# Decoder layer on one core: attention scores transposed by pairs of query tiles, the maximum over keys spread by products of ones with a diagonal

## The reference

```python
q = jnp.einsum('bsd,ed->bse', x, Wq)
k = jnp.einsum('btd,ed->bte', context, Wk)
v = jnp.einsum('btd,ed->bte', context, Wv)
dots = jnp.einsum('bse,bte->bst', q, k) * scale
attn = jax.nn.softmax(dots, axis=-1)
out = jnp.einsum('bst,bte->bse', attn, v)
```

## Time and profile before

| | us |
|---|---|
| median of three runs | 405.06 |
| lowest and highest | 404.93, 406.09 |
| span of the profiled execution | 403.8 |
| attention, from its first score matmul to its last query product | 82.0 to 284.9 |

### The profile page before, as it was taken

One profiled execution on the slowest core, in us unless ns is written; L12 is line 12 of the kernel. 1 busy time (PEld: TensorE's weight loads), 2 busy tenths in 40 slices (PEclk: granted clock), 3 DMA queues, 4 the chain that ended last, 5 costly groups with the idle time before them and its releaser, 6 DMA issues.

```text
span 403.8 us, 7801 instructions
## 1 busy us (share of the span) xinstructions
PE 395.0 (98%) x2584; PEld 367.1 (91%) x2584; DVE 300.1 (74%) x1093; ACT 237.8 (59%) x519; POOL 215.9 (53%) x209
## 2 busy tenths in 40 slices
PE   8999999999999999999999999999999999999877
PEld 7878888899999999999999999999788899999766
DVE  5797768786757867476864848572986989899996
ACT  3886859454764466464545434342557977779462
POOL 1788999764385333153430300000166858989993
PEclk9999999999999999999999999999999969999999
DMA  7900213004434312233211000000100000000102
GB/s 226 310 2 1 83 55 102 8 11 128 128 89 121 118 30 59 58 84 104 65 47 30 2 0 2 1 2 2 27 1 2 0 2 2 28 28 27 41 28 67
DMA packets 19992, 21.38 MB, mean 53 GB/s; under 512 B 3180, under 2 KB 16624, under 8 KB 19952
## 3 DMA queue, kind: packets, MB, share of 16 engines
q1 hardware_dynamic: 18832, 19.96, 16.5%
q10 hardware_dynamic: 1120, 0.92, 0.7%
HBM read 18.78 MB, written 2.10 MB: 52 GB/s over the span
## 4 chain that ended last, share of the span: by engine, by line
PE 80%; POOL 12%; DVE 4%; issue 3%; DMA 1%; ACT 0%; SPq 0%; DVEq 0%; POOLq 0%; ACTq 0%
PE keep_pQ L75 11%; PE keep_pQ L76 11%; PE keep_pQ L77 11%; POOL ffn_prod L1258 9%; PE context_pA L1051 6%; PE context_pA L1053 6%; PE context_pA L1052 6%; PE context_pR L1085 6%; PE context_pR L533 3%; PE context_pA L533 3%; POOL ffn_near L1326 2%; PE ffn_pK L1807 2%; PE context_pR L75 2%; PE context_pR L77 2%; PE context_pR L76 2%
## 5 line engine op out<-in xcount | busy, mean ns | idle before, releaser
L899 DVE TENSOR_TENSOR att_pTl<-context_pR,att_pTh 128x512 fp32r<-128x512 f32 x64 | 36.9, 586 | 29.8 <-ACT att_pTh L811 29.5
L811 ACT ACTIVATE att_pTh<-context_pR 128x512 fp32r<-128x512 f32 x64 | 32.1, 514 | 40.1 <-PE context_pR L1085 40.1
L1258 POOL TENSOR_TENSOR ffn_prod<-ffn_first,ffn_near 128x1024 f32<-128x1024 f32 (+1 forms) x29 | 54.1, 1885 | 2.1 <-DVE ffn_first L1684 2.1
L851 ACT ACTIVATE att_prob<-keep_pQ,att_nmax 128x1206 f32<-128x1206 f32 x16 | 20.3, 1269 | 35.9 <-DVE att_nmax L935 35.8
L930 DVE TENSOR_REDUCE att_mx<-keep_pQ 128x1 f32<-128x402 f32 x64 | 34.5, 564 | 6.9 <-PE keep_pQ L77 6.6
L1837 PE MATMUL ffn_pT<-keep_ident,ffn_prod 128*128 128x128 f32 x240 | 30.5, 283 | 3.7 <-POOL ffn_prod L1258 3.7
L1837 PEld LDWEIGHTS ffn_pT<-keep_ident,ffn_prod 128*128 128x128 f32 x240 | 28.6, 148 | 5.8 <-DVE ffn_hT L1717 4.8
L786 POOL TENSOR_TENSOR keep_rstd<-att_ve,keep_mhalf 128x4 f32<-128x4 f32 x3 | 3.0, 1007 | 55.9 <-DVE att_ve L989 55.9
L1085 PE MATMUL context_pR<-keep_ident,att_prob 128*128 128x128 f32 (+1 forms) x208 | 31.8, 272 | 0.2 <-DVE att_pTl L899 0.2
L1051 PE MATMUL context_pA<-att_pTh,att_cNh 128*128 128x256 f32 (+1 forms) x104 | 31.0, 298 | 0.0
L1051 PE MATMUL context_pA<-att_pTh,context_cNh 128*128 128x256 f32 (+1 forms) x104 | 30.9, 297 | 0.0
(11 more groups left out here) (336 smaller groups left out, 1300.3 us busy)
## 6 DMA issues: line engine op xcount, KB each, us to landing
keep_raw<-in_ctxT SPq DMA_DIRECT2D x24, 256.0 KB, 2.7
keep_raw<-in_ctx SPq DMA_DIRECT2D x24, 256.0 KB, 3.0
out<-keep_x SPq DMA_DIRECT2D x16, 128.0 KB, 1.7
keep_x<-in_x SPq DMA_DIRECT2D x3, 512.0 KB, 9.9
gru_wout<-in_W_out SPq DMA_DIRECT2D x1, 512.0 KB, 8.7
keep_raw<-in_fWq SPq DMA_DIRECT2D x2, 256.0 KB
keep_raw<-in_ctxT SPq DMA_DIRECT2D x8, 32.5 KB, 3.1
keep_raw<-in_ctx SPq DMA_DIRECT2D x4, 65.0 KB
```

The lines of the kernel that those rows point to most:

```text
L811: act.activation(to, bank, ACT.Copy).then_inc(bank_high, 1)
L899: dve.tensor_tensor(to, bank, half(it, 0, n)[0].bitcast(F32), ALU.subtract).then_inc(bank_free, 1)
L1258: return eng.tensor_tensor(prod[:, i % PB, a:b].rearrange("p h (i j) -> p h i j", j=KEYS), (factor if factor is not None else first[:, n % ...
```

## The change

`stage_attention` is rewritten; the other stages are the same. The work goes by pairs p of query tiles (256 columns) and by 7 groups j of two key tiles (the last of one).

- **Scores transposed.** The context stands still, the 256 queries of the pair move, so keys lie on the partitions and a group fills one bank of 512 columns: 12 matmuls a group, 78 a pair. Three banks of pS take turns. No P items are left.
- **Read and maximum.** ScalarE copies each bank to `prob` in SBUF (`read_scores`). VectorE keeps a running maximum over the groups in SBUF (`running_max`), and folds it (`last_max`). TensorE transposes it, VectorE reduces it to a maximum per query and multiplies the identity with it, in halves (`make_shift`); TensorE multiplies a matrix of ones with that diagonal (`spread_shift`), which puts the maximum of each query on all partitions, in the fourth bank.
- **Exponentials.** VectorE subtracts this from `prob` (`shift_scores`), ScalarE raises in place (`raise_scores`) and copies the high half (`probs_high`), VectorE subtracts it from `prob` (`probs_low`): 7 of each a pair.
- **Sums.** GpSimd adds up the groups (`add_up`, `fold`), and two matmuls with a column of ones give the sums (`row_sums`); VectorE inverts them.
- **Order.** TensorE does all scores of pair p, then the values of pair p-1 (`value_group`). The O items of pair p-1 stand in pair p+1, ahead of its score groups 2 and 3. `values_high` and `values_low` of pair p-1 open pair p+1 on ScalarE and VectorE. The ring of pR has two banks instead of three. There is one set of queries, so Q is written after the last scores of its batch.
- **Pieces.** UPTO spreads them over pairs; up to four are early (ScalarE between reads, GpSimd ahead of the additions), the others late (among the exponentials and the additions).

On VectorE, at the end of one pair before: from the maxima of a first tile through the end of its slot to the second tile (att_mx maxima, att_pTl low halves, att_vTl values_low, att_rowsum and att_rinv sums of a row, keep_x output).

The diff, cut to its core:

```diff
+    GROUPS = [range(i, min(i + 2, CT)) for i in range(0, CT, 2)]
     NG = len(GROUPS)
-
-
-
-
-
-
-    PAIRS = TILES // 2
-    EVEN = "O-4 O-3 P0-1 P1-1 P2-1 E S-4 S-3 A0-2 P3-1 A1-2 A2-2 A3-2"
-    ODD = "B0-3 E P0-1 B1-3 P1-1 B2-3 P2-1 B3-3 V-3 P3-1"
-
-    def at_tile(g):
+    BANKS, RING = 3, 2
+    CPIECES = DC * -(-CTX // SEQ)
+    UPTO = (4, 11, 19, 26, 34, 41, 45, 47)
...
+    def before_scores(p, j):
+
         out = []
-        for word in (ODD if g % 2 else EVEN).split():
-            kind, _, back = word.partition("-")
-            a = g - int(back or 0)
-            if 0 <= a < TILES:
-                out.append((kind[0], a, int(kind[1:] or 0)))
-        if g == 0:
-            out += [("X", 1, 0), ("X", 1, 1)]
-        if g == 1:
-            out = [("P", 0, 0), ("P", 0, 1), ("P", 0, 2), ("E", 1, 0), ("Q", 1, 0), ("P", 0, 3), ("Q", 1, 1)]
-        b = (g + 2) // TPB
-        if 2 <= b <= BATCH + 1 and (g + 2) % TPB == 0 and g < TILES or g == TILES:
-            b = BATCH + 1 if g == TILES else b
-            out.insert(out.index(("A", g - 2, 2)), ("X", b, 0))
-            out.insert(out.index(("A", g - 2, 3)), ("X", b, 1))
-        b = (g + 1) // TPB
-        if 2 <= b < BATCH and (g + 1) % TPB == 0:
-            out.insert(out.index(("P", g - 1, 0)), ("Q", b, 0))
-            out.insert(out.index(("P", g - 1, 1)), ("Q", b, 1))
-        if g == TILES:
-            rest = [it for it in out if it[0] not in "EO"]
-            out = rest[:1] + [("F", 0, 0)] + rest[1:2] + [("O", g - 4, 0), ("O", g - 3, 0)] + rest[2:]
-        if g == TILES + 1:
-            out = [it for it in out if it[0] in "BV"] + [("F", 0, 1), ("F", 0, 2)]
-        if g == TILES + 2:
-            out = [("O", g - 4, 0), ("O", g - 3, 0), ("S", g - 4, 0), ("S", g - 3, 0), ("F", 0, 3)]
+        if j in (2, 3) and p >= 2:
+            out.append(("O", 2 * (p - 2) + j - 2, 0))
+        if p % 2 and j in (4, 6):
+            out.append(("X", (p + 1) // 2, (j - 4) // 2))
...
+    def behind_values(p, j):
+
+        if p == PAIRS:
+            return {3: [("X", BATCH + 1, 0)], 4: [("X", BATCH + 1, 1)]}.get(j, [])
+        if p % 2 and p < PAIRS - 1 and j in (3, 4):
+            return [("Q", (p + 1) // 2, j - 3)]
+        return []
...
+    values = [pA[:, 0:COLS], pR[:, 0, 0:COLS]]
+    turned = pS[:, 3, 0:COLS].rearrange("p (t n) -> p t n", n=P)
+    shift = pS[:, 3, COLS:2 * COLS]
+    sums = pS[:, 3, 0:2]
...
+        def add_up(p, j):
+
+            pool.wait_ge(raised, NG * p + j + 1)
+            new = prob[0:rows(j), GROUPS[j][0]:GROUPS[j][-1] + 1]
+            if j == 1:
+                if p >= 1:
+                    pool.wait_ge(part_ready, total_at(p - 1))
+                pool.tensor_tensor(part[:], prob[:, 0:2], new, ALU.add).then_inc(part_ready, 1)
+                return
+            pool.wait_ge(part_ready, part_at(p, j - 1))
+            acc = part[0:rows(j), 0:len(GROUPS[j])]
+            pool.tensor_tensor(acc, acc, new, ALU.add).then_inc(part_ready, 1)
+
+        def fold(p):
+
+            pool.wait_ge(part_ready, part_at(p, NG - 1))
+            if p >= 1:
+                pool.wait_ge(row_mm, sums_at(p - 1))
+            pool.tensor_tensor(total[:], part[:, 0], part[:, 1], ALU.add).then_inc(part_ready, 1)
...
+        def read_scores(p, j):
+
+            act.wait_ge(score_mm, NG * p + j + 1)
+            if p >= 1:
+                act.wait_ge(prob_low, NG * (p - 1) + j + 1)
+                act.wait_ge(part_ready, part_at(p - 1, max(j, 1)))
+            n = len(GROUPS[j])
+            act.activation(prob[0:rows(j), GROUPS[j][0]:GROUPS[j][-1] + 1].rearrange("p c n -> p (c n)"),
+                           pS[0:rows(j), (NG * p + j) % BANKS, 0:n * COLS], ACT.Copy).then_inc(score_read, 1)
+
+        def raise_scores(p, j):
+
+            act.wait_ge(shifted, NG * p + j + 1)
+            s = prob[0:rows(j), GROUPS[j][0]:GROUPS[j][-1] + 1]
+            act.activation(s, s, ACT.Exp, scale=ATT_SCALE).then_inc(raised, 1)
...
+            act.wait_ge(raised, NG * p + j + 1)
+            if p >= 1:
+                act.wait_ge(value_mm, NG * (p - 1) + j + 1)
+            which = slice(GROUPS[j][0], GROUPS[j][-1] + 1)
+            act.activation(pT[0][0:rows(j), which], prob[0:rows(j), which], ACT.Copy).then_inc(prob_high, 1)
...
+        for p in range(PAIRS):
+            if p >= 2:
+                values_high(p - 2)
+            early, late = early_pieces(p), late_pieces(p)
+            for j in range(NG):
+                for it in before_scores(p, j):
+                    if it[0] == "X":
+                        high(it)
+                read_scores(p, j)
+                if early and j in (1, 2, 3, 4):
+                    piece_high(early.pop(0))
+            raise_scores(p, 0)
+            for j in range(NG):
+                if j + 1 < NG:
+                    raise_scores(p, j + 1)
+                probs_high(p, j)
+                for it in behind_values(p, j):
                     high(it)
-            if g <= 2:
-                for i in pieces_at(g):
-                    piece_high(i)
+                if p and j in (2, 4, 5) and late:
+                    piece_high(late.pop(0))
...
-        def row_max(g):
-
-            h = g % 2
-            for j in range(KB):
-                for it in between_scores(g, j):
-                    if it[0] == "O":
-                        output(it[1])
-                    else:
-                        low(it)
-                dve.wait_ge(score_mm, KB * g + j + 1)
-                last = dve.tensor_reduce(mx[:, h, j:j + 1], pS[:, j, 0:min(SPANS[j][1], CTX) - SPANS[j][0]], AX.X,
-                                         ALU.max)
-            at = note(last)
-            dve.wait_ge(dve_chain, at)
-            link(dve.tensor_reduce(tmax[:, h:h + 1], mx[:, h], AX.X, ALU.max))
-            dve.tensor_scalar(nmax[:, h:h + 1], tmax[:, h:h + 1], -ATT_SCALE, None, ALU.mult).then_inc(max_ready, 1)
...
+        def running_max(p, j):
...
+            acc = most[0:rows(j), 0:len(GROUPS[j])]
+            link(dve.tensor_tensor(acc, acc, new, ALU.max))
...
+        def make_shift(p):
+
+            dve.wait_ge(row_mm, turn_at(p))
+            link(dve.tensor_reduce(mx[:], turned, AX.X, ALU.max))
+            link(dve.tensor_tensor(diag[0][:], ident[:].unsqueeze(1).broadcast_to([P, 2, P]),
+                                   mx[:].unsqueeze(2).broadcast_to([P, 2, P]), ALU.mult))
+            for t in range(2):
+                last = dve.scalar_tensor_tensor(out=diag[1][:, t], in0=ident[:], scalar=mx[:, t:t + 1],
+                                                in1=diag[0][:, t].bitcast(F32), op0=ALU.mult, op1=ALU.subtract)
+            last.then_inc(row_dve, 1)
+
+        def shift_scores(p, j):
+
+            if j == 0:
+                dve.wait_ge(row_mm, shift_at(p))
+            n = len(GROUPS[j])
+            s = prob[0:rows(j), GROUPS[j][0]:GROUPS[j][-1] + 1]
+            dve.tensor_tensor(s, s, shift[0:rows(j)].unsqueeze(1).broadcast_to([rows(j), n, COLS]), ALU.subtract)\
+                .then_inc(shifted, 1)
+
+        def probs_low(p, j):
+
+            dve.wait_ge(prob_high, NG * p + j + 1)
+            which = slice(GROUPS[j][0], GROUPS[j][-1] + 1)
+            dve.tensor_tensor(pT[1][0:rows(j), which], prob[0:rows(j), which], pT[0][0:rows(j), which].bitcast(F32),
+                              ALU.subtract).then_inc(prob_low, 1)
...
+        for p in range(PAIRS):
+            if p >= 2:
+                values_low(p - 2)
...
+            last_max(p)
+            make_shift(p)
+            shift_scores(p, 0)
+            shift_scores(p, 1)
+            for j in range(NG):
+                if j + 2 < NG:
+                    shift_scores(p, j + 2)
+                probs_low(p, j)
+                for it in behind_values(p, j):
+                    low(it)
...
+            if p in (2, 4, 6):
+                normalise(p // 2 + 1)
...
+            for m, kt in enumerate(GROUPS[j]):
+                r = CLAST if kt == CT - 1 else P
+                last = split_products(pe, pS[0:r, n % BANKS, m * COLS:(m + 1) * COLS], [
+                    (tuple(c[b % 2][:, k, kt * P:kt * P + r] for c in (cTh, cTl)),
+                     tuple(q[:, k, cols] for q in qT)) for k in range(DC)])
+            last.then_inc(score_mm, 1)
...
+        def turn_max(p):
+
+            pe.wait_ge(row_dve, most_at(p))
+            if p == 0:
+                wait_gates(3)
+            else:
+                pe.wait_ge(row_dve, rinv_at(p - 1))
+            for t in range(2):
+                last = pe.transpose(turned[:, t], top[:, t * P:(t + 1) * P], ident[:])
...
+        def spread_shift(p):
+
+            pe.wait_ge(row_dve, diag_at(p))
+            if p == 0:
+                pe.wait_ge(filled, 2)
+            pe.matmul(shift, onesr[:], diag[0][:].rearrange("p t n -> p (t n)"), start=True, stop=False)
+            pe.matmul(shift, onesr[:], diag[1][:].rearrange("p t n -> p (t n)"), start=False, stop=True)\
```

(24 more changed lines are left out.)

## The result

The changed kernel takes 466.2 us (median of four runs, 464.6 to 467.6), the kernel before 405.4 (four runs, 404.9 to 406.1): a ratio of 1.149, 95% interval 1.146 to 1.153. It is 61 us slower; the forecast was 462, 57 slower, in a range of 425 to 490. The profiled execution has a span of 465.8 us and took 467.6, the longest of the four.

The account below looks back on a forecast made before the run. TensorE, busy 98%, was taken to bound the kernel before; after the change its waits for values_low behind VectorE's queue set the pace. 403.8 plus 49 and 8 for the clock gave 460.8, as a median 462 us, range 425 to 490.

Parts of the forecast that it names:

- TensorE's own work: TensorE's matmuls per pair of query tiles: 20.3 us after the change instead of 22.2, 1.9 less.
- the 399 of the rival: Rival that TensorE stays the bound in attention: a pair takes 20.3 us, the kernel 399 us; chance 0.04.
- The chain: From S, the end of a pair's scores: first shift S+5.1, low halves end S+19.2, then values_low, for which TensorE's output items wait.
- The prediction's signs of it: TensorE waiting 7 to 10 us for values_low in even pairs, low halves 1.0 to 1.3 us, additions 1.5 to 1.8.
- the rival *worse: Rival: running maxima held too, clock 1.2 GHz through scores, 2 to 4 us more per pair, 485 us; chance 0.12.
- Alone they are ... 8.6, to S+13.7: VectorE's shifts and low halves undisturbed by GpSimd: 8.6 us, ending 13.7 us after the end of a pair's scores.
- the exclusion: VectorE's two-SBUF-input low halves and GpSimd's operations take turns, so low halves end at S+19.2 instead of S+13.7.
- the rival *the exclusion does not bite: Rival: GpSimd lets VectorE's low halves pass, so they end at S+13.7; kernel 418 us, chance 0.14.
- Normalise: Four VectorE operations between low halves and values_low, in even pairs and pair 7: 2.0 us taken.
- Q adds 2.8 of work inside that idle time and costs nothing: In odd pairs TensorE's query work, 2.8 us, falls within its wait for values_low and adds no time.
- Clock: TensorE's clock falls behind eight long waits: 0 to 2.3 us each, 0 to 18 in all, 8 taken.
- From the S of pair 0 to that of pair 1: End of pair 0's scores to end of pair 1's: 27 us, with ScalarE waiting for a piece's load until about 115.

Follow-up runs that it names:

- e10: Changed kernel with values, query halves, pieces and first score copies reordered, GpSimd's additions (from pair 1) and piece low halves (third, fourth batch) over 2 columns: 432.4 us.
- e11: Changed kernel in its own order, GpSimd's additions (from pair 1) and piece low halves (third and fourth batch) over 2 columns: 443.0 us.
- e2: Changed kernel with the low half computed as prob minus the shift in PSUM, instead of prob minus the high half in SBUF; additions whole: 450.1 us.
- e4: Changed kernel with 330 extra matmuls filling TensorE's waits for queries and output items, pair 1's wait left unfilled: 455.7 us.
- e5: Changed kernel with values_high and values_low of pair p-1 moved early into pair p, and GpSimd's additions over 2 columns from pair 1 on: 437.6 us.
- e12: Changed kernel with values_high and values_low moved early into pair p and fewer filling matmuls in TensorE's waits: 447.4 us, 1.105 of the kernel before.
- the two further reorderings: Changed kernel with early values, query halves and pieces reordered: 459.5 us; the same with the next pair's first two score copies earlier on ScalarE: 462.4 us.
- e7: Changed kernel, all work kept: values early into pair p, query halves earlier, late pieces spread among exponentials and ahead of additions: 459.5 us.

## Why the prediction was right, point by point

**TensorE's own work.** The forecast had 1.9 us less a pair; with waits everywhere it never set the time. The cadence of 0.117 us that it rests on stayed where the clock was 1.00. But no run reached TensorE's own pace: e10's best S to S is 24.7 us, and what the change would take with all waits gone (the 399 of the rival) stays untested.

**The chain: right.** First shift at S+5.3 (said: 5.1), last low half at S+19.0 (19.2), values_low at S+21.0 (22.0), the output item at once behind it, waits of 6.9 to 8.5 us for att_vTl in even pairs and at the end. The prediction's signs of it came too: low halves at 1.24 us, additions at 1.56, the wait for a copied score group at 104.6 to 111.7 us. The running maxima, which the rival *worse* had held as well, took 0.76 us on average against 0.69: held little.

**But two terms in it were wrong and cancelled.** "Alone they are ... 8.6, to S+13.7": undisturbed they end at S+15.5 (e11). I had counted VectorE's fourteen operations and one first exponential; ScalarE makes an exponential, a high half and often a piece for each group at 0.52 us, 1.57 together, and VectorE waits for it: 0.9 us of the 1.8 are two waits in e11's rows, and 0.2 are the later first shift. And the exclusion was put at 5.5 us a pair (19.2 less 13.7); by the changed kernel against e11 it is 3.5 in pairs 2 and 4 (S+19.0 against S+15.5) and 2.5 to 2.7 in pairs 1, 3 and 5, where e11 ends at S+16.5. That the two errors met at S+19 is luck. So the rival *the exclusion does not bite*, 418, had the wrong price: its case is e11, 443. I had taken 0.40 for ScalarE from the earlier trace rows, and above all I did not lay its queue beside VectorE's. One reading behind the exclusion was loose as well: GpSimd was busy two fifths of the time only in the first stretch of the earlier trace rows, in the last it was under a tenth, while the 0.69 is a mean over the whole stage. e2 settles it.

**Normalise:** 2.0 said, 1.37 measured; e2 shows what it can cost, 4.64. The reason that I gave for the rival, that such an operation is held only little, was wrong.

**"Q adds 2.8 of work inside that idle time and costs nothing": wrong.** In pairs 3 and 5 the output item waited for nothing; TensorE had waited 3.7 us earlier, for the low halves of the queries in the same queue of VectorE, and did sixteen matmuls, 3.4 us, at a clock of 0.50 behind it. S to S from these pairs on is 29.4 and 29.5, for 28.0 and 1 of clock. The size was nearly right, the wait's place was not.

**Clock:** 8 taken, 10.6 measured without pair 1 (e4). The term was right in kind and somewhat small: from the output item to the end of the scores, pair 2 to 3 took 11.8 us instead of the 8.9 and 1 of clock. The span (465.8) is 5.0 over the 460.8 forecast. Of this 1.3 is the later first score matmul, and most of the rest is in such stretches. From the S of pair 0 to that of pair 1 (27 said, 27.8 measured) and from the S of pair 7 to the last query product (38.5 and 1 of clock, 39.5 measured) the sum was right, and so was the load in pair 1.

**How much each cause holds.** Taken alone: GpSimd's additions 23.6 us, the place of the values 13.9, the clock 10.6. Together they give less than their sum (e5: 28.6 for 37.5; e12: 18.8 for 24.5). The waits that come up in their place (keep_x, queries, loads) account for it in kind; in e12 some of the clock was also left, behind the unfilled 3.1 us. With GpSimd's work gone the order still costs 27 to 37 us, and the rest of it is a row of places in three queues (outputs behind running maxima, query halves, ScalarE's pace, start and end). How it divides among them was not taken apart.

## What to carry to other kernels

When an operation moves from PSUM to two inputs in SBUF, price it at its duration beside a busy GpSimd, and price the other engine's queue too: here the additions of that engine held 24 us. Lay the queues of all engines for one period side by side, and let the slowest of them at each step set the pace, rather than sum one engine. A wait taken away shows the next one: early values were expected to gain 44 us and gained 14, and the two further reorderings, expected to gain 20 and 11 more, lost 7 and gained nothing.

## What the runs showed of the hardware

A tensor_scalar of 256 columns with one tensor in SBUF took 0.34 us with GpSimd nearly idle (e11) and 1.16 beside GpSimd's additions and subtractions (e2), a two-input subtraction of 512 columns 0.69 (e11) and 1.24 (changed kernel). GpSimd pays as well: additions took 1.29 us where the low halves read PSUM (e2) and 1.56 beside two-input low halves, and the short one of 65 rows and 256 columns took 2.19 us beside the normalise of pair 2 and 0.72 at best (e7). So of the same two operations, normalise and what GpSimd has beside it, GpSimd's lost in the changed kernel and normalise in e2.
